# A graph attention kernel: first edges of node groups found on two levels, keys made in two parts, and statistics of x moved behind two tiles of one-hots

## What is computed

```
def gat_layer(x, src, dst, W, a_src, a_dst, b):
    h = x @ W
    e = leaky_relu((h @ a_src)[src] + (h @ a_dst)[dst], 0.2)
    ex = exp(e - segment_max(e, dst)[dst])
    alpha = ex / segment_sum(ex, dst)[dst]
    return segment_sum(alpha[:, None] * h[src], dst) + b

h = relu(layernorm(x));  h = relu(gat_layer(h, W1: 128 -> 256));  x = x + gat_layer(h, W2: 256 -> 128)
h = relu(layernorm(x));  x = x + gat_layer(h, W3: 128 -> 128)
```

## Time and profile before

| what | value |
|---|---|
| three runs, median (lowest to highest) | 775.45 us (774.66 to 776.54) |
| the profiled execution's own time | 774.95 us |
| its span, first to last instruction | 773.2 us |
| first phase (windows, keys, counts) | 0 to 244.5 us |
| the three layers | 244.5 to 773.2 us |
| busy over the span: DVE, PE, ACT, POOL | 703.8, 665.6, 505.3, 371.1 us |
| mean granted TensorE clock | 0.942 of full speed |

### The profile page before, as it was taken

The page is one execution under the profiler, slowest core; times in us unless marked ns, Lnnn a source line. Parts: engine busy times, 40 slices in busy tenths (PEclk is TensorE's granted clock), DMA queues, the critical chain, the costliest instruction groups (busy, mean ns, idle before and its releaser), DMA issues.

```text
span 773.2 us, 14598 instructions
## 1 busy us (share of the span) xinstructions
PE 665.6 (86%) x5692; PEld 648.0 (84%) x5692; DVE 703.8 (91%) x915; ACT 505.3 (65%) x732; POOL 371.1 (48%) x343
## 2 busy tenths in 40 slices
PE   4345989898886989999999997999988989998994
PEld 4345888898885989999989997999988889998984
DVE  5499999999975999999999989899998989999994
ACT  0044344444436998778776687788785789787880
POOL 1504000000003566455476577586677866885873
PEclk9997788898866999999999999999999999999998
DMA  3400000000002222222123323222123223323211
GB/s 97 119 0 1 1 1 1 2 1 1 1 1 8 82 94 88 80 84 76 47 65 91 114 58 97 84 71 76 50 60 70 99 58 79 108 93 117 78 58 38
DMA packets 50016, 45.39 MB, mean 59 GB/s; under 512 B 13329, under 2 KB 47866, under 8 KB 49941
## 3 DMA queue, kind: packets, MB, share of 16 engines
q1 hardware_dynamic: 49140, 43.13, 19.4%
q0 software_dynamic: 800, 1.26, 0.6%
HBM read 31.33 MB, written 13.05 MB: 57 GB/s over the span
## 4 chain that ended last, share of the span: by engine, by line
PE 27%; DVE 23%; issue 7%; DMA 5%; ACT 3%; POOL 2%; DVEq 0%; SPq 0%; POOLq 0%
PE ps L1635 22%; DVE ps L928 11%; DVE scratch L1006 6%; DMA scratch<-counts_bf 2%; DVE ps L930 2%; DMA g_lines<-g_row 1%; DVE mu L940 1%; PE ps L1688 1%; DMA gathered<-g_lines 1%; ACT scratch L1400 1%; POOL scratch L656 1%; PE ps L1666 1%; PE ps L1643 1%; ACT scratch L1346 1%; PE ps L1658 1%
## 5 line engine op out<-in xcount | busy, mean ns | idle before, releaser
L1635 PE MATMUL ps<-hB,scratch 125*125 125x129 f32 x3450 | 406.7, 277 | 28.6 <-DVE scratch L1006 22.6
L1635 PEld LDWEIGHTS ps<-hB,scratch 125*125 125x125 f32 x3450 | 392.5, 189 | 37.8 <-DVE scratch L1006 30.0
L656 POOL TENSOR_TENSOR scratch<-scratch 125x625 f32<-125x625 f32 x197 | 262.1, 1339 | 153.3 <-ACT scratch L1406 143.3
L928 DVE SCALAR_TENSOR_TENSOR ps<-C,a_unit,ps 125x625 f32<-125x625 uint8 x330 | 277.3, 865 | 2.1
L1406 ACT ACTIVATE scratch<-scratch,r_src 125x625 f32<-125x625 f32 x197 | 178.4, 905 | 4.7
L1400 ACT ACTIVATE scratch<-gathered,r_inv 125x625 f32<-125x625 f32 x197 | 159.1, 808 | 33.0 <-PE ps L1635 26.1
L1570 PE MATMUL ps<-scratch 128*128 128x125 bf16 x1250 | 148.6, 296 | 25.1 <-DVE scratch L842 18.9
L1570 PEld LDWEIGHTS ps<-scratch 128*128 128x128 bf16 x1250 | 143.0, 121 | 29.6 <-DVE scratch L842 23.2
L1006 DVE SCALAR_TENSOR_TENSOR scratch<-ps,r_src,C 125x625 f32<-125x625 f32 x178 | 152.9, 859 | 10.1 <-PE ps L1619 9.4
L1280 ACT ACTIVATE C<-ps 125x1750 uint8<-125x1750 f32 (+3 forms) x50 | 74.1, 1487 | 96.9 <-PE ps L1570 96.9
L842 DVE TENSOR_TENSOR scratch<-key_lo,hB 128x6656 bf16<-128x6656 bf16 (+3 forms) x26 | 94.6, 3640 | 4.5 <-PE ps L1570 4.5
(11 more groups left out here) (146 smaller groups left out, 445.8 us busy)
## 6 DMA issues: line engine op xcount, KB each, us to landing
scratch<-counts_bf SPq DMA_DIRECT2D x142, 152.6 KB
counts_bf<-scratch SPq DMA_DIRECT2D x73, 152.6 KB
gathered<-g_lines SPq DMA_DIRECT2D x14, 305.2 KB
xr<-in_x SPq DMA_DIRECT2D x1, 1562.5 KB
out<-xr SPq DMA_DIRECT2D x5, 312.5 KB
edge_sb<-in_edges SPq DMA_DIRECT2D x1, 805.7 KB
gathered<-ext_lines SPq DMA_DIRECT2D x5, 122.1 KB
w<-in_W SPq DMA_DIRECT2D x2, 128.0 KB
```

Source lines behind the costliest of these rows:

```text
L656: g.tensor_tensor(slot[s], slot[s], wide[r % WIDE], ALU.mult).then_inc(pool_done, 1)
L928: v.scalar_tensor_tensor(dest, counts, unit[:, s:s + 1], top, ALU.min, ALU.max).then_inc(S.top_done, 1)
L1635: last = mm(ps[0:P, acc_at(t):acc_at(t) + HW], A[:, P * t:P * (t + 1)], feat, start=opens and t in (0, 3), stop=closes, skip_group_check=True)
```

## The change

- `x` is loaded behind the weights, and only when `starts_ok` is raised.
- The windows' first edges are found on two levels. One comparison with each partition's first sample (`after_first`) is multiplied, in five fp32 products with 26 columns, with `steps`: 25 columns with the difference of each sample to the next partition's (made by one product with the new constant `step_up` and one ACT copy) and a column of ones. This gives for every window the samples of the one partition in which it starts, and the partition's number; DVE compares and adds those (five small instructions in place of two). The 25 comparisons and 125 products are gone.
- The first gather has a semaphore of its own, and its keys are made alone (`keys(0, 1)`, 256 slots). Then come `one_hots(0)`, `one_hots(1)`, the statistics of x, the keys of the other four groups (`keys(1, 5)`, 1024 slots), and `one_hots(2)`. The keys k_lo and k_dl are written into `gathered` in place, k_hi and k_ok to `hB`.
- PE sums `covered` between `count(0)` and `count(1)`, where it waits for all keys, and transposes the keys of group c + 1 ahead of the third tile of chunk c; ACT copies them there. `one_hots` of the first tile of each chunk waits for them.
- ACT normalises x five tiles at a time, one tile ahead of each chunk's `features`. POOL's addition of b2 now waits for all five parts, the last in chunk 4.

```diff
@@ block.sync
             sp.dma_start(edge_sb[:, :, :], edges.rearrange("(p k) c -> p k c", p=P)).then_inc(edges_in, 16)
-            sp.dma_start(xr[:, :, :], x_v).then_inc(x_in, 16)
...
             sp.dma_start(b3r[:, :], b3.unsqueeze(0).broadcast_to([P, D])).then_inc(weights_in, 16)
+            sp.wait_ge(starts_ok, 1)
+            sp.dma_start(xr[:, :, :], x_v).then_inc(x_in, 16)
@@ block.gpsimd
+            g.affine_select(out=step_up, in_=ident[0:P, 0:P], compare_op=ALU.not_equal, fill=-1.0, base=1,
+                            pattern=[[-1, P]], channel_multiplier=1).then_inc(consts, 1)
...
-                                     ).then_inc(gather_in, 16)
+                                     ).then_inc(gather_in if i else first_in, 16)
...
-            pool.wait_ge(g0_ready, 1)
+            pool.wait_ge(g0_ready, NC)
             g.tensor_tensor(xr[:, :, :], xr[:, :, :], b2r[:, :].unsqueeze(1).broadcast_to([P, T, D]),
@@ block.vector
-            for k in range(NS):
-                v.tensor_scalar(before[:, k, :], win_dst, sampled[:, k:k + 1], None,
-                                ALU.is_gt).then_inc(before_ok, 1)
+            v.tensor_scalar(after_first, win_dst, sampled[:, 0:1], None, ALU.is_gt).then_inc(before_ok, 1)
             dve.wait_ge(before_sum, 1)
-            v.tensor_scalar(start_f[:, :], ps[0:P, CNT:CNT + WG], float(SAMPLE), float(1 - SAMPLE),
-                            ALU.mult, ALU.add).then_inc(start_lin, 1)
+            picked = ps[0:P, CNT:CNT + 32 * WG].rearrange("p (g k) -> p g k", g=WG)
+            v.tensor_tensor(below, picked[:, :, 0:NS], win_base[:, :].unsqueeze(2).broadcast_to([P, WG, NS]),
+                            ALU.is_lt).then_inc(start_lin, 1)
+            v.tensor_reduce(start_f[:, :], below, AX.X, ALU.add).then_inc(start_lin, 1)
+            v.scalar_tensor_tensor(start_f[:, :], picked[:, :, NS], float(NS), start_f[:, :], ALU.mult,
+                                   ALU.add).then_inc(start_lin, 1)
+            v.tensor_scalar(start_f[:, :], start_f[:, :], float(SAMPLE), float(1 - SAMPLE - SAMPLE * NS),
+                            ALU.mult, ALU.add).then_inc(start_lin, 1)
...
+            def keys(g0, g1):
+                hi, lo, dl, ok, src, dst = (plane[:, g0:g1, :] for plane in (k_hi, k_lo, k_dl, k_ok, src_i, dst_i))
...
+            dve.wait_ge(first_in, 16)
+            keys(0, 1)
             one_hots(0)
-            dve.wait_ge(keys_ok, 3)
             one_hots(1)
+            node_statistics()
+            dve.wait_ge(gather_in, 16 * (WG - 1))
+            keys(1, WG)
+            one_hots(2)
             dve.wait_ge(covered_sum, 1)
@@ block.scalar
+            act.wait_ge(steps_ps, 1)
+            a_.activation(steps[:, 0:NS], ps[0:P, DIF:DIF + NS], ACT.Copy).then_inc(steps_sb, 1)
...
             for c in range(NC):
                 for j in range(CT):
+                    if c < NC - 1 and j == 2:
+                        copy_keys(c + 1)
+                    if j == FEAT_AT[c] - 1:
+                        normalise_first(c)
@@ block.tensor
-            for k in range(NS):
-                pe.wait_ge(before_ok, k + 1)
-                for g in range(WG):
-                    last = mm(ps[0:P, CNT + g:CNT + g + 1], before[:, k, P * g:P * (g + 1)], ones_b[:, :],
-                              start=(k == 0 and g == 0), stop=(k == NS - 1), skip_group_check=True)
+            mm(ps[0:P, DIF:DIF + NS], step_up, sampled[:, :], start=True, stop=True).then_inc(steps_ps, 1)
+            pe.wait_ge(before_ok, 1)
+            pe.wait_ge(steps_sb, 1)
+            for g in range(WG):
+                last = mm(ps[0:P, CNT + 32 * g:CNT + 32 * g + NS + 1], after_first[:, P * g:P * (g + 1)], steps,
+                          start=True, stop=True)
...
+            def sum_covered():
+                pe.wait_ge(keys_ok, 6)
...
             def features(c):
                 pe.wait_ge(half_out[0], c * CT + FEAT_AT[c] + 1)
-                if c == 0:
-                    pe.wait_ge(g0_ready, 1)
-                    pe.wait_ge(flag_ok, 1)
+                pe.wait_ge(g0_ready, c + 1)
+                if c < NC - 1:
+                    pe.wait_ge(keys_sb, 2 * c + 4)
...
             for c in range(NC):
                 for j in range(CT):
+                    if c == 0 and j == 1:
+                        sum_covered()
+                    if c < NC - 1 and j == 2:
+                        transpose_keys(c + 1)
```

More of the change, by code:

```diff
@@ L199, in gat_stack_kernel @@
         at += WIDE * WIDE_COLS
-        assert at <= 2 * OH and g_at + 1280 + U * 3 * P <= 2 * OH and NS * NW <= 4 * OH
+        assert at <= 2 * OH and g_at + 1280 + U * 3 * P <= 2 * OH
         ps = ctx.enter_context(nc.psum_tensor("ps", [128, 8 * 512], fp32))
@@ L237, in gat_stack_kernel @@
         dve_consts = sem("dve_consts")
-        samples_ok = sem("samples_ok")
         before_ok = sem("before_ok")
+        steps_ps = sem("steps_ps")
+        steps_sb = sem("steps_sb")
+        first_in = sem("first_in")
         before_sum = sem("before_sum")
@@ L795, in _ @@
             v.memset(hA[:, :, D:HW], 1.0).then_inc(h_ones, 1)
-            dve.wait_ge(x_in, 16)
-            for t in range(T):
-                last = v.bn_stats(bn6[:, t, :], xr[:, t, :])
-            last.then_inc(F.ln_lin, 1)
-            dve.wait_ge(F.ln_lin, 1)
-            for t in range(T):
-                last = v.bn_aggr(mv[:, t, :], bn6[:, t, :])
-            last.then_inc(F.ln_stats, 1)
-            dve.wait_ge(gather_in, 16 * WG)
-            src, dst = gath4[:, :, :, 0], gath4[:, :, :, 1]
@@ L902, in inverse_r @@
                 v.reciprocal(r_inv[L % 2][:, t0:t1], r_src[L % 2][:, t0:t1]).then_inc(rinv_ready, 1)
-            for t in range(2, T - 1):
+            for t in range(3, T - 1):
                 one_hots(t)
@@ L1256, in _, with copy_keys, normalise_first @@
             a_.activation(w3[:, D:AW], ps[:, VEC + 6:VEC + 8], ACT.Copy).then_inc(prep_done, 1)
-            for i, (key, minus) in enumerate(((key_lo, 0.0), (key_col, -1.0))):
-                act.wait_ge(keys_T, i + 1)
-                for k in range(KC):
-                    last = a_.activation(key[:, :, 0:P, k],
-                                         tiles(KEYS[i] + 128 * WG * k, WG, rows=128), ACT.Copy, bias=minus)
-                last.then_inc(keys_sb, 1)
-            act.wait_ge(before_sum, 1)
-            act.wait_ge(F.ln_ready, 1)
-            for t in range(T):
-                last = a_.activation(hA[:, t, 0:D], xr[:, t, :], ACT.Relu, bias=nbias[:, t:t + 1],
-                                     scale=rstd[:, t:t + 1])
-            last.then_inc(g0_ready, 1)
+            def copy_keys(g):
+                for i, (key, minus) in enumerate(((key_lo, 0.0), (key_col, -1.0))):
+                    act.wait_ge(keys_T, 2 * g + (2 if g else i + 1))
+                    a_.activation(key[:, g, 0:P, :].rearrange("p w k -> p k w"),
+                                  tiles((KEYS_AT if g else KEYS0)[i], KC, rows=128), ACT.Copy, bias=minus).then_inc(keys_sb, 1)
+            copy_keys(0)
+            def normalise_first(c):
+                if c == 0:
+                    act.wait_ge(before_sum, 1)
+                    act.wait_ge(F.ln_ready, 1)
+                for t in range(c * CT, (c + 1) * CT):
+                    last = a_.activation(hA[:, t, 0:D], xr[:, t, :], ACT.Relu, bias=nbias[:, t:t + 1],
+                                         scale=rstd[:, t:t + 1])
+                last.then_inc(g0_ready, 1)
             def counts_out(c, j):
```

98 lines of the change are left out of this document (59 added, 39 removed).

## The result

The changed kernel takes 765.05 us (median of 4 runs, 764.39 to 766.27) against 776.0 us of the kernel before in the same comparison: ratio 0.9863, 95% interval 0.9844 to 0.9883. That is 10.9 us. The forecast was 767.6 us, 0.990 of the 775.45 us that stood on record for the kernel before.

What follows compares the result with a forecast made beforehand. DVE's queue was taken to bound the kernel until the layers; -15.6 + 5.0 + 0.6 + 2.4 = -7.6 us from 774.95 gave 767.35, stated as 767.6 us. Its own range was 764.5 to 770, the wider range 761 to 772.

Steps and rivals of the forecast that it cites:

- the power holds nobody: Rival at POOL's power beside DVE's second keys: it delays no DVE instruction, -12.6 us, 763 us; chance 0.20.
- the first gather is slowed: Rival at the first gather beside x's load: landing at 26 us, not 22; -3.6 us, 771.5 us; chance 0.13.
- Part 1, the start: From the samples' landing to starts_ok: ready at 14.2 us against 24.54, 10.3 us earlier (9.4 to 11.3).
- Part 2, the first gather: First gather beside x: 6.4 us plus 0.4 for x, keys' data landing at 22.1 us; x at 36 us.
- Part 3, DVE's list: DVE's keys, one-hots and statistics up to the end of one_hots(2): 61.6 us against 77.23, 15.6 us earlier.
- Part 4, the power: POOL's scale and bias, mostly the power, beside the keys of four groups: holds DVE 5.0 us.
- Part 5, behind the mark: From the end of one_hots(2) to the first layer: one_hots(4) waits 0.6 us, b2's addition makes the extremes 2.4 late.

Runs made afterwards that it cites:

- e1: The changed kernel with x loaded only when the first gather has landed; 764.25 us, a single run.
- e2: The changed kernel with the load of x split into 112 and 13 partitions; 768.45 us, a single run.
- e8: The changed kernel with edges and x split, x behind the edges, statistics back in the first gather's wait, b2 added in the first layer; 757.84 us.
- e9: e8 with PE's and ACT's preparation of the weights moved behind the transposes and copies of the first group's keys; 752.68 us.
- e3: The changed kernel with the power made a second time by POOL, reaching beside the one-hots; 764.83 us, a single run.
- e4: The changed kernel with a plain POOL addition of 125x1536 elements ahead of the power, beside the second part of the keys; 770.08 us, a single run.
- e5: The kernel before with only the start on two levels, x still behind the edges, keys in one list; ratio 0.9982 to the kernel before.
- e10: The changed kernel with the first group's keys waiting for all five gathers; 769.76 us, a single run.
- e6: The changed kernel with the addition of b2 taken out of the one-hots and made in five parts in the first layer; 764.37 us.
- e11: e9 with the addition of b2 put back as one POOL instruction in chunk 4; 754.45 us.

## Why the prediction came out right

The time, 765.05 us, lies in the range and within the forecast's own one, but two steps of the sum were wrong, one by +2.7 and one by -5.0 us, and that they half cancelled is luck. What came is the two rivals "the power holds nobody" and "the first gather is slowed" at once. Two of the prediction's own signs of being wrong appeared: DVE waited for the first gather until 25.62 us, with 24 as the bound, and the layers differ by 1.4 us, with 1 as the bound; the second of these is within their spread over unchanged kernels. In its own order:

- **Part 1, the start.** From the samples to the starts 4.75 us against 4.44: the five products took 2.27 us, near the upper of the two ends and not 2.0. The edges landed at 10.21 and not 9.76 in this execution; over the kernels with one edge load that varied from 9.45 to 10.53. Together 0.8 us late.
- **Part 2, the first gather: the step failed.** It put 6.4 + 0.4 us; measured were 9.5. The base was too long (e1: 5.4 without x) and the meeting with x ten times too cheap (4.1, not 0.4); neither the 0.4 nor the rival's 4 was worked out from a row. b3r was read as "neither queue starves the other", without a price: it let PE go on 7.8 us after its issue among the gathers, and 4.6 after in the changed kernel with no gather there. The rival "slowed" with its 4 us had the right size. The rule of the Trainium skill that the prediction cites for it (DMA: Bandwidth & Descriptors, Queues, rings and completion order: a packet of many descriptors from one ring before the next) points the same way, and so does e2; how long such a turn is no run here shows. x landed later than said, near 39 us and not 36 (the DMA share is 0.24 from 38 to 39 us and 0 after), but DVE, held up by the gather, came only at 42.42.
- **Part 3, DVE's list.** Keys 2.81 us (2.9), two tiles 13.99 (14.1), statistics 6.63 (6.7), keys of four groups 8.76 (8.7). All terms held. The statistics on the path are the price that the changed order pays; in e8 and e9 they lie ahead of the first keys, which start right behind them. When the gather had landed there isn't seen, so whether the whole price is gone stays open.
- **Part 4, the power: the step failed.** 5.0 us were put in; 0 came. From the row with L656 and L946 it took that any POOL instruction holds DVE for its whole length. e3, e4 and e9 show that the addition does and the power doesn't. The rival "the power holds nobody", given 0.20, is what happened. Stated as the Trainium skill has it, SBUF — State Buffer, section Who interferes with whom, the loser blocks for the full instruction; the addition agrees (4.44 us against 1.23 in e4), the power doesn't (1.21 us beside it), and the measurement decides. POOL, in turn, did wait: L606 took 5.12 us here and 4.37 undisturbed.
- **Part 5, behind the mark.** `one_hots(4)` waited 0.25 us (0.6 predicted), and the waits for PE at the chunks' ends grew by 0.3 us together. The turn: one instruction of 10.11 us, extremes at 219.43 where the 11.6 us gained by 209.39 would have them at 217.2: 2.3 us lost against 2.4. By the row of `ab`, which was ready at 216.1, it is 3.3: PE was through with the attention terms sooner than before.
- **The sum.** Up to the first layer -9.1 us against -7.6: +0.8 (start) + 2.7 (gather) - 5.0 (power) = -1.5. The rest of the difference between 767.6 and 765.05 is 1 us: the layers were 1.4 us shorter, and the median lies 0.66 us over the profiled execution and not 0.25. The layers vary by more than that from profile to profile.

What is shown: the meeting of x and gather (e1, e2), the addition's hold and the power's lack of one (e3, e4), that the earlier start alone brings nothing while x lies beside the gathers (e5), that not waiting for the other gathers is worth 5.2 us at the mark and 4.1 at the first layer (e10), the turn's stall (e6, e11). That the power reads and writes only at its ends is a guess that e3 and e4 allow, not seen. Among executions DVE's waits for PE between the mark and the turn differ by about 1 us, so a smaller difference at the first layer says nothing.

## What to carry to other kernels

A shorter step ahead of a transfer is worth only what the transfers behind it let through: look at what else is on the queues at the new, earlier time, and run the shortened step alone once. The load of 125 partitions left most of the DMA engines idle (share 0.31); splitting it into 112 + 13 cut the wait for the edges by a third. But x split in the same way delayed the gather beside it still more, so keep such a load and a small gather apart. Between GpSimd and VectorE don't take the length of a GpSimd instruction for its price: look for a row of the same operation beside a VectorE instruction, or make one.

## What the runs showed of the hardware that was not expected

- The first of five indirect gathers of 125 rows of 2 KB needs 5.4 us from its issue until VectorE goes on when no load is beside it (e1), 9.5 us beside x (DMA share of both 0.49), and 12.35 us beside x in two pieces (share 1.22, e2). For all five the load costs less: 12.9 us from the first issue before, 14.9 beside x (e10).
- GpSimd's power of 25 numbers a partition, 4.4 us long, doesn't delay a VectorE instruction with two inputs in SBUF (3.62 us beside it as ever, e3 and e9), while an addition of 1536 numbers delays the same kind by 3.2 us (e4).
- In the other direction short GpSimd instructions do wait when VectorE is in the middle of one of its own: the first scale instruction, 0.33 us undisturbed before, takes 0.65 beside a key instruction, the power 5.12, and in e9 another instruction of 0.33 us takes 3.18 beside one-hots.
